# Attention scores computed twice, the second time with keys on partitions, the row maximum added in PSUM and the sums taken by a matrix of ones

## The chip, the cores and the metric

The kernel runs on one core of a Trainium2 chip. The metric is the device time of one execution in microseconds (us). Three executions of the kernel before gave a median of 409.12 us (408.9 to 410.25).

## The reference

One decoder layer on x of 8 batches x 128 tokens x 128 features, all in float32. In order: a bidirectional state-space (Mamba) block, residual and layer norm (x1); a cross attention of 16 heads of 8 features whose queries come from x1 and whose keys and values come from a context of 8 x 128 x 128, residual and layer norm (x2); a mixture of 8 experts with one expert a token, residual and layer norm. The part that the change touches is

```python
Q, K, V = query @ Wq.T, key @ Wk.T, value @ Wv.T      # split into 16 heads of 8
scores = einsum('bqhd,bkhd->bhqk', Qh, Kh) / sqrt(8)
attn = softmax(scores, axis=-1)
out = einsum('bhqk,bkhd->bqhd', attn, Vh) @ Wo.T
```

## The kernel before

Each engine has its own hand-written program (sync, gpsimd, scalar, tensor, vector: L315, L369, L476, L663, L997). They meet through semaphores. The eight PSUM banks are handed out by a written plan (L209 to L238): each entry names a tile and its bank, TensorE waits in `to_fill` until the bank's last tile was read, readers wait in `to_read`, and `filled` and `was_read` count both sides.

The scan of the state-space block takes most of the time and ends at about 254 us of the span. Then come the first norm, the attention, the routing (gate logits, counts, slots), the scatter of tokens to memory by GpSimd (L465), the experts, the gather (L471) and the last norm.

The attention has 16 tiles, i = 0 to 15: tile i is batch i // 2 and half c = i % 2 of the heads, 8 heads of 128 queries x 128 keys. The loop index i of every engine runs to LAST, and the stages of one tile lie in successive turns i. Heads are numbered h = 4 g + j: group g is a block of 32 feature rows, j one of its four heads. A head's 8 features are picked by masks: `k_maskT` holds the keys four times, each with the rows of one j only (L606), and `q_maskT` holds the queries four times, each with the rows of one g only (L1180 on VectorE, L615 on ScalarE), so one matmul of K = 128 gives four heads.

Per tile, before:

- TensorE, `scores` (L875): two matmuls of 128x128 weights and 512 columns into two banks, queries on partitions.
- VectorE, `shift_scores` (L1186): row maximum over PSUM (L1195), then scores minus maximum into SBUF (L1196).
- ScalarE (L625 to L630): eight exponentials of 128x128, each with its row sum (L628).
- VectorE, `invert_sums` (L1199): reciprocal of 8 numbers a partition (L1201). GpSimd multiplies the tile by them (L457).
- TensorE, `turn_probs` (L888): eight transposes (their line is that of the helper `turn`, L666). ScalarE copies them to SBUF (L639).
- TensorE, `weigh_values` (L895): eight matmuls of 32 output partitions each, so four lie side by side in the array (L903). For every second tile ScalarE copies the result (`evacuate`, L479) and TensorE multiplies by Wo (L957). VectorE adds the residual (L1256) and takes the moments (L1156, L1157).

In TensorE's program each float32 matmul shows as two passes, each with its own weight load, and a transpose as one.

The routing follows: `normalize` (L1162), transposes and logits (L918), `choose_expert` (L1206), `count_tokens` (L921), `place_tokens` (L1221). Among the lines of other stages that are used below are L745 (four projections with 9 rows of weights, each from its own block of 32 partitions), L727 (the matmuls behind them), L1047 (a copy of 8 numbers a partition), L1168 (the residual of the first norm) and L1070 (the start of VectorE's work after the convolution).

## Time and profile before

| | us |
|---|---|
| median of 3 executions (lowest, highest) | 409.12 (408.9, 410.25) |
| the profiled execution | 410.48 |
| its span, first to last instruction | 408.6 |
| TensorE / VectorE / ScalarE / GpSimd busy | 311.5 / 294.2 / 264.6 / 233.7 |
| mean granted TensorE clock (1 is 2.4 GHz) | 0.901 |

The durations below come from the one profiled execution. Engines are PE (TensorE matmuls), PEld (its weight loads), DVE (VectorE), ACT (ScalarE), POOL (GpSimd), SP (SyncE). Busy time is no measure of what bounds a stage: that is read from the chain of waits and from who stands idle.

### The profile page before, as it was taken

What the parts mean: (1) busy time and instruction counts of PE and PEld (TensorE: products, weight loads), DVE (VectorE), ACT (ScalarE), POOL (GpSimd) and SP (SyncE); (2) the same over time, 40 slices, a digit from 0 to 9 for tenths busy, and PEclk for the clock granted to TensorE, in tenths of its full rate; (3) what the DMA queues carried; (4) which work ended last, traced back from release to release, by engine and by line L of the source; (5) the groups of instructions that cost most, each with busy time, mean ns of one, the idle gap of its engine ahead of it and who ended that gap; (6) DMA issues with size and microseconds to landing.
All of it is one profiled execution on the core that took longest, in us unless ns stands there. A gap on an engine that the chain in (4) does not pass through costs nothing.

```text
span 408.6 us, 5591 instructions
## 1 busy us (share of the span) xinstructions
PE 311.5 (76%) x1688; PEld 189.0 (46%) x1688; DVE 294.2 (72%) x454; ACT 264.6 (65%) x677; POOL 233.7 (57%) x148
## 2 busy tenths in 40 slices
PE   4999400589999999899999999978899965249800
PEld 3443200564545555445555454834466654239700
DVE  2540579679999999999999997769777745301335
ACT  3348761059999999899999996459899972003200
POOL 7100499349888888888888882115445451700063
PEclk9999655599999999999999999999999998559955
DMA  7966001103323333222222100000000000120122
GB/s 172 315 180 209 0 1 52 51 2 103 103 105 103 109 103 105 102 92 88 97 97 97 48 2 1 2 2 0 2 1 2 3 2 0 45 72 16 34 54 65
DMA packets 16769, 26.92 MB, mean 66 GB/s; under 512 B 1964, under 2 KB 10308, under 8 KB 16740
## 3 DMA queue, kind: packets, MB, share of 16 engines
q1 hardware_dynamic: 16036, 25.46, 19.6%
q0 software_dynamic: 704, 1.10, 1.0%
q8 instruction: 14, 0.23, 0.2%
q14 instruction: 15, 0.12, 0.1%
HBM read 24.00 MB, written 2.56 MB: 65 GB/s over the span
## 4 chain that ended last, share of the span: by engine, by line
DVE 41%; PE 34%; issue 8%; ACT 7%; POOL 4%; DMA 3%; DVEq 1%; POOLq 0%; SPq 0%; ACTq 0%
DVE arena L1104 26%; PE bank L666 10%; PE bank L884 5%; DVE acc L1114 5%; PE bank L705 3%; PE bank L978 3%; PE bank L752 2%; ACT arena L628 2%; DVE delta L1085 2%; PE bank L986 2%; PE bank L957 2%; POOL dispatched_tokens L465 2%; PE bank L694 2%; POOL arena L471 2%; PE bank L903 2%
## 5 line engine op out<-in xcount | busy, mean ns | idle before, releaser
L435 POOL TENSOR_TENSOR arena<-arena,k_maskT 128x1024 f32<-128x1024 f32 x64 | 152.8, 2408 | 29.1 <-DVE arena L1104 29.1
L1104 DVE TENSOR_TENSOR_SCAN arena<-bank,arena 128x512 f32<-128x512 f32 x128 | 146.5, 1213 | 0.0
L666 PE MATMUL bank<-ident,arena 128*128 128x128 f32 (+1 forms) x686 | 103.0, 285 | 30.4 <-DVE arena L1104 11.1
L666 PEld LDWEIGHTS bank<-ident,arena 128*128 128x128 f32 (+1 forms) x686 | 75.2, 142 | 97.6 <-DVE arena L1104 60.9
L557 ACT ACTIVATE bank<-delta,a_neg 128x508 f32<-128x508 f32 x128 | 88.5, 692 | 29.5 <-DVE arena L1104 24.4
L804 PE MATMUL bank<-conv_in_T,ident 128*128 128x512 f32 x192 | 92.8, 593 | 0.0
L568 ACT ACTIVATE conv_in_T<-bank,c_col 128x256 f32<-128x256 f32 x192 | 80.4, 473 | 11.5 <-PE bank L666 10.7
L457 POOL TENSOR_TENSOR arena<-arena,rsum 128x1024 f32<-128x1024 f32 x16 | 30.3, 1897 | 36.9 <-DVE rsum L1201 36.9
L628 ACT ACTIVATE arena<-arena 128x128 f32<-128x128 f32 x128 | 37.7, 296 | 7.0 <-DVE arena L1196 6.9
L804 PEld LDWEIGHTS bank<-conv_in_T,ident 128*128 128x128 f32 x192 | 31.6, 191 | 15.8 <-issue 15.0
L884 PE MATMUL bank<-k_maskT,uT 128*128 128x512 f32 x64 | 30.9, 607 | 1.4 <-DVE uT L1180 0.8
L1008 DVE COPY arena<-bank 128x160 f32<-128x160 f32 (+2 forms) x20 | 8.1, 433 | 31.9 <-PE bank L986 16.5
L752 PE MATMUL bank<-diag_d,uT 128*128 128x128 f32 x64 | 10.0, 334 | 26.0 <-DVE woutT L1008 26.0
L1114 DVE SCALAR_TENSOR_TENSOR acc<-bank,c_col,acc 128x256 f32<-128x256 f32 x64 | 27.6, 479 | 2.6 <-PE bank L666 2.6
L1195 DVE TENSOR_REDUCE rmax<-bank 128x8 f32<-128x1024 f32 x16 | 19.5, 1217 | 12.8 <-PE bank L666 7.4
L471 POOL DMA_INDIRECT arena<-expert_outputs,take_u x8 | 7.6, 952 | 34.4 <-DMA expert_outputs<-arena 32.3
L418 POOL TENSOR_SCALAR arena<-arena 128x1024 f32<-128x1024 f32 x2 | 7.3, 3638 | 34.8 <-ACT arena L512 34.8
L479 ACT ACTIVATE arena<-bank 128x512 f32<-128x512 f32 (+1 forms) x18 | 10.3, 578 | 22.8 <-PE bank L666 18.6
L628 ACT ACTIVATION_READ_ACCUMULATOR arena<-arena 128x1 f32 x128 | 23.9, 187 | 0.0
L752 PEld LDWEIGHTS bank<-diag_d,uT 128*128 128x128 f32 x64 | 9.8, 248 | 26.4 <-issue 26.4
L1196 DVE TENSOR_TENSOR arena<-bank,rmax 128x1024 f32<-128x1024 f32 x16 | 19.6, 1224 | 0.5
L639 ACT ACTIVATE arena<-bank 128x1024 f32<-128x1024 f32 x16 | 16.1, 1004 | 2.0 <-PE bank L666 2.0
(155 smaller groups left out, 343.7 us busy)
## 6 DMA issues: line engine op xcount, KB each, us to landing
k_maskT<-b_rows SPq DMA_DIRECT2D x32, 512.0 KB, 3.7
w_sb<-in_L_ffn_w SPq DMA_DIRECT2D x1, 2048.0 KB, 10.3
dispatched_tokens<-zeros SPq DMA_DIRECT2D x1, 640.0 KB, 15.6
expert_outputs<-arena SPq DMA_DIRECT2D x4, 160.0 KB, 2.1
x_tok<-in_x SPq DMA_DIRECT2D x1, 512.0 KB, 3.9
ctx_tok<-in_ctx SPq DMA_DIRECT2D x1, 512.0 KB, 4.2
out<-arena SPq DMA_DIRECT2D x2, 256.0 KB, 2.3
arena<-dispatched_tokens SPq DMA_DIRECT2D x1, 384.0 KB, 3.8
```

Of the source, the lines that this page charges most:

```text
L435: gp.tensor_tensor(dBx[g % 2][h], du[:, dr, h, :], b_bc[:, g % RING, :], ALU.mult).then_inc(dBx_ok, 1)
L457: gp.tensor_tensor(prob[i % 3], prob[i % 3], rsum[:, i % 3, :].unsqueeze(2).to_broadcast([P, CH, S]), ALU.mult).then_inc(prob_ok, 1)
L557: sc.activation(tiles(bank[:, k % DA_BANKS, :], HB)[:, :, inner], tiles(delta[:, dr, h, half(q)], HB)[:, :, inner], ACT.Exp, scale=a_neg[: ...
L568: sc.activation(y_part[:, p, at:at + DI], hT(g, b), ACT.Copy, scale=c_col[:, dr, b, n:n + 1]).then_inc(part_ok, 1)
L628: last = sc.activation(prob[i % 3][:, h, :], prob[i % 3][:, h, :], ACT.Exp, scale=SCALE, accum_out=rsum[:, i % 3, h:h + 1])
L666: return pe.transpose(dst, src, ident[0:src.shape[0], 0:src.shape[0]])
L752: last = pe.matmul(dst[:, P * n:P * n + P], uT[:, dr, h, S * b:S * b + S], diag_d[:, dr, h, :], start=(n == 0 and dr == 0), stop=False, sk ...
L804: last = pe.matmul(bank[:, Y_BANK + p, :], ident[:, :], y_part[:, p, :], start=False, stop=False, skip_group_check=True)
L884: last = pe.matmul(bank[:, g, :], q_maskT[:, g, S * b:S * b + S], k_maskT[:, b, :, :].rearrange("p j k -> p (j k)"), start=True, stop=True)
L1104: ve.tensor_tensor_scan(o, a, v, 0.0, ALU.mult, ALU.add).then_inc(scanned, 1)
L1114: ve.scalar_tensor_tensor(acc[:, b, :], hT(g, b), c_col[:, dr, b, n:n + 1], acc[:, b, :], ALU.mult, ALU.add).then_inc(acc_ok, 1)
L1196: was_read(f"s{i}", ve.tensor_tensor(prob[i % 3], src, rmax[:, c, :].unsqueeze(2).to_broadcast([P, CH, S]), ALU.subtract))
```

## The change

The softmax is built so that the probabilities come out with keys on partitions, as the product with V needs them.

- The scores of `scores` serve the maximum alone. Their operands are now blocks of 32 partitions (`rows_g`) of an unmasked `qT` (in place of `q_maskT`, L157) and of `k_maskT`, so K = 32. They use banks 0 and 1 for every tile, where before tiles alternated between two pairs.
- VectorE takes the row maxima only (`row_maxima`). TensorE transposes them (`turn_max`, one transpose a tile) and ScalarE copies them negated to `neg_max`.
- TensorE computes the scores again, keys on partitions (`shifted_scores`): eight matmuls of K = 32 and 128 columns, then eight more of K = 32 that add the negated maximum of each query with weights `head_row`, whose only nonzero row is that of the head.
- ScalarE takes one exponential of 128x1024 from PSUM to SBUF.
- TensorE multiplies by V as before, and again by a 128x32 matrix of ones, which gives the sums in the layout of the output (one bank, 6, for every batch). VectorE takes the reciprocal of 128x512 sums and multiplies once a batch (`divide_by_sums`).
- Gone are the shift, the masks of the queries, the products on GpSimd, the eight transposes a tile and their copies. The output product moves a turn later, and the routing of the first half moves into the loop. A few constants are made at the start on VectorE and before the attention on GpSimd.

```diff
-        plan += [("x1T0", 6), ("q0", 4), ("x1T1", 7), ("s0", 0, 2), ("q1", 7), ("s1", 2, 2)]
+        plan += [("x1T0", 6), ("q0", 4), ("x1T1", 7), ("q1", 5)]
+        for i in range(LAST + 1):
+            if i < TILES_A:
+                plan += [(f"s{i}", 0, 2)]
+            if 1 <= i <= TILES_A:
+                plan += [(f"m{i - 1}", 7)]
+            if 2 <= i < TILES_A + 2:
+                plan += [(f"e{i - 2}", 2, 2)]
+            if i % 2 == 1 and 3 <= i < TILES_A + 3:
+                plan += [(f"av{i // 2 - 1}", 4 + (i // 2 - 1) % 2), (f"sum{i // 2 - 1}", 6)]
+            if i % 2 == 0 and 6 <= i < TILES_A + 6:
+                plan += [(f"wo{i // 2 - 3}", 7)]
...
# gpsimd
+            gp.memset(row_max[:, :, :, :], 0.0).then_inc(v_zero, 1)
+            gp.memset(ones_32[:, :], 1.0).then_inc(v_zero, 1)
             rstds(0)
-            for i in range(2 * B):
-                gp.wait_ge(sums_ok, i + 1)
-                gp.tensor_tensor(prob[i % 3], prob[i % 3], rsum[:, i % 3, :].unsqueeze(2).to_broadcast([P, CH, S]),
-                                 ALU.mult).then_inc(prob_ok, 1)
# scalar
+            evacuate("q1", qT[:, half(1)])
+            for i in range(1, LAST):
+                if i <= TILES_A:
+                    if i >= 3:
+                        to_read(sc, f"e{i - 3}")
+                    evacuate(f"m{i - 1}", neg_max[:, (i - 1) % 2, :], lambda ap: ap[:, 0:S], scale=-1.0)
+                if 2 <= i < TILES_A + 2:
+                    n = i - 2
+                    to_read(sc, f"e{n}")
...
+                    was_read(f"e{n}", sc.activation(probT[n % 3].rearrange("p h q -> p (h q)"),
+                                                    bank[:, 2:4, :].rearrange("p a t -> p (a t)"), ACT.Exp, scale=SCALE))
# tensor
                 for g in (2 * c, 2 * c + 1):
-                    last = pe.matmul(bank[:, g, :], q_maskT[:, g, S * b:S * b + S],
-                                     k_maskT[:, b, :, :].rearrange("p j k -> p (j k)"), start=True, stop=True)
+                    rows_g = slice(32 * g, 32 * g + 32)
+                    last = pe.matmul(bank[:, g - 2 * c, :], qT[rows_g, S * b:S * b + S],
+                                     k_maskT[rows_g, b, :, :].rearrange("p j k -> p (j k)"), start=True, stop=True)
...
+            def turn_max(i):
+                wait_read(pe, f"s{i}")
+                dst = to_fill(pe, f"m{i}")
+                filled(f"m{i}", turn(dst[:, 0:S], row_max[:, i % 2, :, :].rearrange("p g j -> p (g j)")))
+            def shifted_scores(i):
+                b, c = i // 2, i % 2
+                to_fill(pe, f"e{i}")
+                wait_read(pe, f"m{i}")
+                for j in range(GH):
+                    for g in (2 * c, 2 * c + 1):
+                        rows_g = slice(32 * g, 32 * g + 32)
+                        pe.matmul(bank[:, 2 + g - 2 * c, S * j:S * j + S], k_maskT[rows_g, b, j, :],
+                                  qT[rows_g, S * b:S * b + S], start=(j == 0), stop=False, skip_group_check=True)
+                for j in range(GH):
+                    for g in (2 * c, 2 * c + 1):
+                        rows_g = slice(32 * g, 32 * g + 32)
+                        last = pe.matmul(bank[:, 2 + g - 2 * c, S * j:S * j + S], head_row[rows_g, j, :],
+                                         neg_max[rows_g, c, :], start=False, stop=True, skip_group_check=True)
+                filled(f"e{i}", last)
...
+                for h in range(CH * c, CH * c + CH):
+                    g, j = h // GH, h % GH
+                    last = pe.matmul(total[32 * j:32 * j + 32, S * g:S * g + S], ones_32[:, :],
+                                     probT[i % 3][:, h % CH, :], start=True, stop=True)
...
             for i in range(LAST):
+                if i < TILES_A:
+                    scores(i)
+                if 1 <= i <= TILES_A:
+                    turn_max(i - 1)
+                if 2 <= i < TILES_A + 2:
+                    shifted_scores(i - 2)
+                if 3 <= i < TILES_A + 3:
                     weigh_values(i - 3)
-                if i % 2 == 1 and 5 <= i < 2 * B + 5:
-                    b = i // 2 - 2
+                if i % 2 == 0 and 6 <= i < TILES_A + 6:
+                    b = i // 2 - 3
...
+                if i == ROUTE0 + 1:
+                    count_tokens(0)
# vector
+            link(ve.tensor_reduce(one_of_32[:, :], ident[:, :].rearrange("p (g r) -> p r g", r=32)[:, 0:GH, :],
+                                  AX.X, ALU.add))
+            for j in range(GH):
+                ve.tensor_copy(head_row[:, j, :], one_of_32[:, j:j + 1].to_broadcast([P, S])).then_inc(head_row_ok, 1)
...
+            evacuate("q0", qT[:, half(0)])
+            def row_maxima(i):
+                c = i % 2
+                to_read(ve, f"s{i}")
+                ve.wait_ge(v_zero, 3)
                 if i >= 2:
+                    to_read(ve, f"m{i - 2}")
+                src = bank[:, 0:2, :].rearrange("p a (j k) -> p a j k", j=GH)
+                was_read(f"s{i}", ve.tensor_reduce(row_max[:, c, 2 * c:2 * c + 2, 0:GH], src, AX.X, ALU.max))
+            def divide_by_sums(b):
+                was_read(f"sum{b}", ve.reciprocal(inverse[:, :], to_read(ve, f"sum{b}")))
+                wait_read(ve, f"sum{b}")
+                if b >= 2:
+                    to_read(ve, f"wo{b - 2}")
+                src = to_read(ve, f"av{b}")
+                was_read(f"av{b}", ve.tensor_tensor(outT[b % 2], src, inverse[:, :], ALU.mult))
...
             for i in range(LAST + 1):
+                if i < TILES_A:
+                    row_maxima(i)
+                if i % 2 == 1 and 5 <= i < TILES_A + 5:
+                    divide_by_sums(i // 2 - 2)
                 if i % 2 == 0 and 6 <= i < TILES_A + 6:
...
+                if i == ROUTE0 - 2:
                     normalize(res2, x2, 1, 0, x2_ok)
                 if i == ROUTE0:
                     evacuate("x2T0", x2T[:, half(0)])
+                if i == ROUTE0 + 1:
+                    choose_expert(0)
+                if i == ROUTE0 + 2:
+                    place_tokens(0)
             normalize(res2, x2, 1, 1, x2_ok)
-            place_tokens(0)
```

ROUTE0 goes from 2B + 3 = 19 to 2B + 2 = 18; TILES_A is 16.

## Rows read from the trace of the kernel before

**Rows 1.** Stretches: us; busy (count) of PE, PEld, DVE, ACT, POOL; PE clock; DMA.

```profile
266.80:294.20 27.40, 22.48 (x123) 11.27 (x124) 21.34 (x29) 21.20 (x106) 10.27 (x6) 1.00 0.00 1
294.20:324.70 30.50, 30.50 (x259) 19.53 (x258) 23.02 (x37) 28.72 (x141) 15.17 (x8) 1.00 0.01 2
324.70:343.10 18.40, 13.31 (x153) 10.01 (x152) 8.54 (x23) 11.51 (x42) 6.93 (x5) 1.00 0.00 1
```

**Rows 2.** The chain of waits, two tiles of the steady stretch: start, us, what.

```profile
301.00 1.09 PE bank L957 x8
302.09 1.72 PE bank L884 x4
303.81 0.87 PE bank L666 x8
304.69 0.57 PE bank L903 x16
305.26 1.91 PE bank L884 x4
307.17 0.87 PE bank L666 x8
308.05 0.57 PE bank L903 x16
```

**Rows 3.** Groups in 266.8 to 343.1 us: count | busy us, mean ns | idle before, releasers.

```profile
L628 ACT ACTIVATE arena<-arena 128x128 f32<-128x128 f32 x128 | 37.7, 296 | 7.0 <-DVE arena L1196 6.9
...
L1195 DVE TENSOR_REDUCE rmax<-bank 128x8 f32<-128x1024 f32 x16 | 19.5, 1217 | 12.8 <-PE bank L666 7.4 <-issue 3.1 <-PE bank L884 2.3
...
L639 ACT ACTIVATE arena<-bank 128x1024 f32<-128x1024 f32 x16 | 16.1, 1004 | 2.0 <-PE bank L666 2.0
```

**Rows 4.** TensorE in order of time, 35.6 to 37.9 us.

```profile
35.66 1.14 PE L745 MATMUL bank<-rows,dtT 9*128 9x512 f32 x8
36.73 1.54 PE L727 MATMUL bank<-uT,xprojT 128*105 128x512 f32 x3
```

**Rows 5.** Single lines of VectorE: duration ns min/median/max; L1047 as a group.

```profile
L1201 DVE RECIPROCAL rsum<-rsum x16: 191/191/203, 277.2 to 332.6; 128x8 f32<-128x8 f32 x16
...
L1243 DVE RECIPROCAL route_b<-route_b x2: 178/178/179, 347.5 to 353.3; 128x4 f32<-128x4 f32 x2
...
L1047 DVE COPY vec_cols<-bank 128x8 f32<-128x8 f32 x1 | 0.2, 157 | 0.0
...
L1168 DVE TENSOR_TENSOR arena<-bank,x_tok x2: 657/674/691, 260.3 to 262.6; 128x512 f32<-128x512 f32 x2
...
332.62 0.20 DVE L1201 RECIPROCAL rsum<-rsum 128x8 f32<-128x8 f32 x1 [2.40 <-ACT arena L628]
```

**Rows 6.** In order of time, the start of the attention.

```profile
268.80 0.66 PE L666 MATMUL bank<-ident,x_tok 128*128 128x128 f32 x4 [0.85 <-DVE x_tok L1162]
...
270.21 1.95 PE L884 MATMUL bank<-k_maskT,uT 128*128 128x512 f32 x4 [0.75 <-DVE uT L1180]
...
271.25 0.60 ACT L479 ACTIVATE arena<-bank 128x512 f32<-128x512 f32 x1
...
272.20 1.22 DVE L1195 TENSOR_REDUCE rmax<-bank 128x8 f32<-128x1024 f32 x1 [2.14 <-PE bank L884]
```

**Rows 7.** VectorE in order of time, its work after the last output product.

```profile
341.62 0.69 DVE L1008 COPY arena<-bank 128x512 f32<-128x512 f32 x1 [2.11 <-PE bank L666]
342.23 0.28 DVE L1256 TENSOR_TENSOR arena<-bank,x_tok 128x128 f32<-128x128 f32 x1
...
342.87 0.18 DVE L1157 BATCH_NORM_AGGREGATE moments<-stats 128x2 f32<-128x6 f32 x1
343.53 0.19 DVE L1212 TENSOR_REDUCE route_b<-bank 128x4 f32<-128x32 f32 x1 [0.47 <-PE bank L918]
...
344.63 0.60 DVE L1162 TENSOR_SCALAR ctx_tok<-arena,moments,rstd 128x128 f32<-128x128 f32 x2
```

**Rows 8.** VectorE in order of time, its first work after the convolutions.

```profile
39.88 0.69 DVE L1070 TENSOR_SCALAR arena<-arena 128x1024 f32<-128x1024 f32 x1 [14.53 <-ACT arena L512]
```

More of the change, by code:

```diff
@@ L155, in decoder_layer_kernel @@
         x1T = arena[:, 9, :]
-        q_maskT = uT[:, :, :, :].rearrange("p a h t -> p (a h) t")
-        prob = [arena[:, c, :].rearrange("p (h k) -> p h k", h=CH) for c in range(3)]
-        probT = [arena[:, 3 + c, :].rearrange("p (h k) -> p h k", h=CH) for c in range(2)]
-        outT = [arena[:, 6, BANK * c:BANK * c + BANK] for c in range(2)]
+        qT = uT[:, 0, 0, :]
+        probT = [arena[:, c, :].rearrange("p (h q) -> p h q", h=CH) for c in range(3)]
+        inverse = arena[:, 3, 0:BANK]
+        outT = [arena[:, 4, BANK * c:BANK * c + BANK] for c in range(2)]
         res2 = arena[:, 8, :].rearrange("p (b d) -> p b d", b=B)
@@ L609, in _ @@
                          lambda ap: tiles(ap, HB * HEADS))
-            sc.wait_ge(q_first_ok, 1)
-            src = to_read(sc, "q0")
-            for g in range(2, HEADS // GH):
-                last = sc.activation(q_maskT[:, g, half(0)], src, ACT.Copy, scale=group_mask[:, g:g + 1])
-            was_read("q0", last)
             evacuate("x1T1", x1T[:, half(1)])
@@ L898, in weigh_values @@
                 wait_read(pe, f"v{b // HB}")
-                wait_read(pe, f"pT{i}")
-                dst = bank[:, where[f"av{b}"][0], :] if c else to_fill(pe, f"av{b}")
+                wait_read(pe, f"e{i}")
+                dst = bank[:, where[f"av{b}"][0], :]
+                total = bank[:, where[f"sum{b}"][0], :]
+                if not c:
+                    to_fill(pe, f"av{b}")
+                    to_fill(pe, f"sum{b}")
                 for h in range(CH * c, CH * c + CH):
@@ L903, in weigh_values @@
                     last = pe.matmul(dst[32 * j:32 * j + 32, S * g:S * g + S], v_pad[:, b, h, :],
-                                     probT[c][:, h % CH, :], start=True, stop=True)
-                if not c:
+                                     probT[i % 3][:, h % CH, :], start=True, stop=True)
+                if c:
+                    filled(f"av{b}", last)
+                for h in range(CH * c, CH * c + CH):
+                    g, j = h // GH, h % GH
+                    last = pe.matmul(total[32 * j:32 * j + 32, S * g:S * g + S], ones_32[:, :],
+                                     probT[i % 3][:, h % CH, :], start=True, stop=True)
+                if c:
+                    filled(f"sum{b}", last)
+                else:
                     last.then_inc(av_half, 1)
-                else:
-                    filled(f"av{b}", last)
             def gate_logits(g):
@@ L1175, in _ @@
             normalize(res1, x1, 0, 1, x1_ok)
-            def mask_queries(th, groups):
-                src = to_read(ve, f"q{th}")
-                for g in groups:
-                    last = ve.tensor_scalar(q_maskT[:, g, half(th)], src, group_mask[:, g:g + 1], None, ALU.mult)
-                return last
-            mask_queries(0, range(2)).then_inc(q_first_ok, 1)
-            def shift_scores(i):
+            evacuate("q0", qT[:, half(0)])
+            def row_maxima(i):
                 c = i % 2
                 to_read(ve, f"s{i}")
-                src = bank[:, 2 * c:2 * c + 2, :].rearrange("p a (j k) -> p (a j) k", j=GH)
-                if i >= 3:
-                    to_read(ve, f"pT{i - 3}")
+                ve.wait_ge(v_zero, 3)
                 if i >= 2:
-                    wait_read(ve, f"s{i - 2}")
-                link(ve.tensor_reduce(rmax[:, c, :], src, AX.X, ALU.max))
-                was_read(f"s{i}", ve.tensor_tensor(prob[i % 3], src, rmax[:, c, :].unsqueeze(2).to_broadcast([P, CH, S]),
-                                                   ALU.subtract))
-            def invert_sums(i):
-                ve.wait_ge(exp_ok, i + 1)
-                ve.reciprocal(rsum[:, i % 3, :], rsum[:, i % 3, :]).then_inc(sums_ok, 1)
+                    to_read(ve, f"m{i - 2}")
[8 more added lines that the diff above has]
+                was_read(f"av{b}", ve.tensor_tensor(outT[b % 2], src, inverse[:, :], ALU.mult))
             def over_e(ap):
@@ L1246, in _ @@
             for i in range(LAST + 1):
[L1247 to L1253 removed]
+                if i < TILES_A:
+                    row_maxima(i)
+                if i % 2 == 1 and 5 <= i < TILES_A + 5:
+                    divide_by_sums(i // 2 - 2)
+                if i % 2 == 0 and 6 <= i < TILES_A + 6:
                     b = i // 2 - 3
```

92 lines of the change are left out of this document (21 added, 71 removed).

## The prediction

> **What bounds the kernel now.** I read the stretches first, then the chain of waits inside them, then the groups and single lines for prices. The attention runs from about 267 to 343 us. In its middle TensorE is busy for the whole 30.50 us at full clock, while VectorE and GpSimd have slack and ScalarE is close to full [rows 1]. The chain there is TensorE alone: one period is scores 1.72, transposes 0.87, values 0.57, scores 1.91, transposes 0.87, values 0.57, output product 1.09, together 7.61 us for two tiles [rows 2]. So an operation taken from ScalarE, VectorE or GpSimd earns nothing there unless TensorE is relieved too. Only the start and the end, where TensorE idles (22.48 of 27.40 and 13.31 of 18.40 us [rows 1]), could be helped by the other engines.
>
> **Prices on TensorE.** A transpose is one pass of 0.109 us (0.87 for 8). The values are 16 passes, four side by side: 4 x 0.109 is 0.44, the row has 0.57, so entering that shape costs about 0.12. Scores behind values take 1.91 instead of 1.72: entering the full shape costs 0.19. I take 0.20 for every other change of shape. The output product is then 1.09 less 0.20, for 8 passes of 0.111 [rows 2]. Do blocks of 32 rows run side by side? Four matmuls of 512 columns from four blocks started at 35.66 and the next line started at 36.73: 1.07 us, which is one change (0.2) and two passes of 0.43, not eight [rows 4]. They do, at least with 512 columns. The granted clock stays a thing to watch, since it was 1.00 throughout [rows 1].
>
> Per turn, after:
> - Scores, K = 32, two blocks side by side: 0.20 + 2 x 0.43 = 1.06 (before 1.72 or 1.91).
> - Transpose of the maxima: 0.20 + 0.11 = 0.31. The eight transposes (0.87) go.
> - Shifted scores: 16 matmuls are 32 passes, in 16 pairs: 0.20 + 16 x 0.111 = 1.98. New. This is the one shape that no row shows (32 rows, 128 columns). Its lower bound is 0.109 a pair, which changes nothing. Above, either each pass waits for its weights, about 0.21 a pair (the 0.11 and half the cost of a change), or the blocks don't overlap, 0.22 a pair. I take 0.111, as rows 4 show overlap and rows 2 show hidden loads.
> - Values and sums: 0.12 + 8 x 0.11 = 1.0 (before 0.57).
> - Output product, every second turn: 1.09, as before.
>
> An odd turn is 4.35 and an even one 5.44, so TensorE alone needs 9.79 us for two tiles where it needed 7.61.
>
> The Trainium skill, page "TensorE: Matmul & The Clock Gate", Part 3 (row and column tiling), says that a weight load overlaps running matmuls only where the row group differs. In rows 2 the output product loads full-height weights for each of its 8 passes at 0.111 a pass, so loads of the same row group are hidden here, and the page would give the 0.21 above.
>
> **The new wait.** There is one bank for the sums. The first half of the next batch's values and sums (odd turns) must wait until the reciprocal of the last batch has read it. In VectorE's program that reciprocal stands behind the maxima of the same turn, which stand behind that turn's scores. So an odd turn can't be shorter than scores 1.06, hand-over 0.2 (270.21 + 0.2 + 1.71 of passes against 272.20 [rows 6]), maximum 1.2 [rows 3], reciprocal R, values and sums 1.0: 3.5 + R. It is longer than TensorE's own 4.35 once R is over 0.9.
>
> **R, the reciprocal of 128x512.** The rows have it only with 8 and 4 numbers. By medians, (191 - 178) / 4 is 3.3 ns a number; against a copy of 8 numbers it is (191 - 157) / 8, 4.3 ns above the copy's own 1 ns or so, 5.3 ns; and where the engine had stood waiting for it, as it had for the 4 numbers, the 8 took 203: (203 - 178) / 4 is 6.3 ns [rows 5]. The last compares like with like, so R = 0.2 + 504 x 0.0063, rounded to 3.3 us. The bounds: as cheap as any operation of 512 numbers, 0.67 [rows 5]; 3.3 ns gives 1.85; from above, all of the 203 beyond the copy's fixed 150 gives 6.6 ns, 3.5 us.
>
> With R = 3.3 an odd turn is 6.8 us, two tiles 12.2.
>
> **The sum, in the times of the trace.**
> - Start. The masks of the queries go, but the second half's queries now stand before the first scores: x1T1 turned by 269.5 [rows 6], copy 0.6 [rows 6], queries 1.0, hand-overs: turn 0 starts at 271.2, a us later than now (270.21).
> - Turns 0 and 1 are serial, as there is one pair of banks for the scores: 2 x (1.06 + 0.2 + 1.2) = 5.0. Turn 2 is 3.35, turn 3 4.35: 283.9. Turn 4: 288.3.
> - Six odd turns of 6.8 and five even ones of 5.44: 68.0. Turn 16 begins at 356.3 and takes 4.4 (no scores): 360.7.
> - Turn 17: VectorE adds and takes moments (0.8 [rows 7]), normalises (1.1), then R, then 1.0 of values: with hand-over 6.4, 367.1. Turn 18: rest of values 0.9, output 1.1, then on VectorE 0.8 and the copy 0.7 [rows 7]: 370.8.
> - Turn 19: R and the product 0.7 [rows 5]: 374.8. `choose_expert(0)` 1.1 (343.53 to 344.63 [rows 7]) and the counts 0.4 now stand before the last output product, 1.1: 377.4. Add and moments: 378.4. Before, they ended at 343.05 [rows 7]: 35.3 later.
> - Then `place_tokens(0)` (about 2.1) stands before the last normalisation where GpSimd's 1.6 did: 0.4 more. Scatter, experts and gather follow unchanged.
>
> That is +35.7 us. **Costed at nothing**: the five small operations of VectorE at the start, whose cover is 14.53 us of idleness (without it 1.5 us) [rows 8]; two memsets of GpSimd, which waits there for the moments; ScalarE's turn, one small copy and one exponential of 1.0 against eight of 0.296 with their sums and a copy [rows 3]. SP's queue is not touched. With R hidden it would be 8 x (3.3 - 0.9) less: 6 odd turns, turn 17 and turn 19 carry it.
>
> The profiled execution, 410.5 (span 408.6 and 1.9 around it), goes to 446; it lies 1.4 above the median, so from 409.1 I forecast 445.
>
> **Rivals.**
> - A, the forecast: R of 2.7 to 3.6 and pairs of blocks side by side, 440 to 448. Chance 0.53.
> - B, a short reciprocal, up to 2.2 us. The medians of 191 and 178 speak for it. With 1.85 it is 12 less, 433; at 0.9 and below TensorE bounds, 425. Chance 0.20.
> - C, a long reciprocal: eight ordinary steps a number. An ordinary number costs about 1.04 ns (1024 in 1.2 us [rows 3], less the fixed part), so eight are 8.3 ns, R = 4.4, 9 us more, 454. Against it: 8 numbers would lie 33 ns above 4, and lie 13 to 25 above. Chance 0.09. The Trainium skill, page "VectorE: DVE Perf Modes", "First, the fixed hardware budget", says that the reciprocal runs its divide steps with a repeat count of 8.
> - D, the pairs aren't side by side at 128 columns, or wait for their weights. Loads exposed: 1.6 more in turns 2, 3, 4 and the even ones up to 16, nine in all (in odd turns it hides in R), 0.1 more in each turn's scores: +16, 461. No overlap: 9 x 1.8 and 16 x 0.86: +30, 475. Chance 0.10.
> - E, faster. TensorE's changes of shape cost nothing with small weights, and a pair of 32-row passes takes half a pass (0.055). The even turn is then 0.86 + 0.11 + 0.88 + 0.88 + 0.89 = 3.6 and the odd one 3.6 + 0.2 at the least, if R is 0.7: 7.5 for two tiles, below 7.61, and it decides only there. With the shorter end (turns 17 to 19 in 8 us instead of 16.7) about 406. Rows 2 show changes at 0.12 to 0.20 and rows 4 a full 0.43 for a pass of few rows. Chance 0.02.
> - The rest, such as a clock that falls in TensorE's 2.5 us waits: 0.06, on the slow side.
>
> **How the numbers follow.** About 0.3% (1.2 us) can be told from no change. The likeliest case gives 445. The range is 421 to 461: it takes in B, A, C and the first half of D; outside are E, the worse half of D and most of the rest. Slower 0.97, same 0.01, faster 0.02.
>
> **What would show it.** In the changed profile: eight reciprocals of 128x512 of about 3.3 us; TensorE waiting some 2.5 us before the first half of the values in odd turns, its releaser the reciprocal; 12.2 us for two tiles, 5.4 of them the even turn; no busy GpSimd; ScalarE at about 1.3 us a tile. Wrong if the reciprocals are below 2.2 us, if TensorE has no gap in mid-stretch, if shifted scores take over 2.5 us, if the granted clock is under 1.00 between 272 and 370, or if the last moments lie before 365.

## The result, and the profile after

The changed kernel takes 486.71 us (median of 4 runs, 483.79 to 488.73) against 409.01 (408.72 to 410.25): a ratio of 1.1875, 95% interval 1.183 to 1.192. The forecast was 445, with 461 as its upper end: slower was right, the size was not, and the time lies 26 us outside the range. The profiled execution took 483.79 us, with a span of 482.0; its own forecast was 446. TensorE's mean granted clock over the span fell from 0.90 to 0.81. Of two kernels below (one full-height product more, and the first scores at full height with the ring kept) three runs in four are 1.5 to 2.2% longer than the fourth, so differences from these two are taken from their fastest run.

The stretches of the attention, cut where the granted clock changes. The columns are the stretch, its length, then busy time and instructions of the engines, the granted clock, and DMA:

```profile
core 0: us, PE busy (x) PEld busy (x) DVE busy (x) ACT busy (x) POOL busy (x), PEclk, DMA share, GB/s
266.80:272.10 5.30, 3.57 (x11) 1.03 (x11) 1.55 (x2) 0.91 (x3) 0.00 (x0) 1.00 0.00 0
272.10:313.00 40.90, 39.38 (x323) 28.01 (x325) 11.06 (x9) 6.71 (x11) 0.00 (x0) 0.50 0.00 1
313.00:319.90 6.90, 4.46 (x71) 3.22 (x73) 5.87 (x6) 1.30 (x2) 0.00 (x0) 0.99 0.01 2
319.90:330.10 10.20, 10.20 (x79) 7.55 (x81) 1.55 (x3) 1.30 (x2) 0.00 (x0) 0.50 0.01 2
330.10:336.90 6.80, 4.36 (x71) 3.11 (x71) 5.63 (x5) 1.30 (x2) 0.00 (x0) 1.00 0.00 0
```

Before, this stretch had 1.00 throughout [rows 1]. Now the clock falls to its lower level (1.2 GHz) at 272.1, four us after the first scores. It stays there for 41 us, and then goes up and down once per pair of tiles. To the last moments at 415.3 it is at half for 102 us. "PE busy" hides it: a pass at half clock counts as busy for about twice as long (the scores of a turn are 2.01 us below, where the forecast has 1.06).

The chain of waits, first at half clock, then at full clock (start, length, what; the lines are the scores L873, transposed maxima L657, shifted scores L890, maximum added L895, values L911, sums L917, output product L972, reciprocal L1209). It answers to [rows 2]:

```profile
286.26 2.01 PE bank L873 x4
288.27 0.41 PE bank L657
288.68 2.01 PE bank L890 x16
290.69 1.71 PE bank L895 x16
292.39 1.01 PE bank L911 x16
293.40 0.85 PE bank L917 x16
...
310.88 2.01 PE bank L972 x8
312.88 1.18 PE bank L873 x4
...
315.23 3.36 DVE arena L1209
318.59 0.14 issue
318.72 0.64 PE bank L911 x16
319.37 0.44 PE bank L917 x16
```

The turn at half clock takes 8.00 us (286.26 to 294.26); the forecast has 4.35 for its work. The odd turn at full clock, from 312.88 to 319.80, is the forecast's: 6.92 against 6.8, with the maximum and the reciprocal in it.

The groups of the attention, 268 to 420 us (count | busy, mean ns | idle before, releaser), and all reciprocals as single lines; they answer to [rows 3, 5]:

```profile
L890 PE MATMUL bank<-uT,k_maskT 32*128 32x128 f32 x256 | 27.7, 379 | 0.0
L1205 DVE TENSOR_REDUCE row_max<-bank 128x8 f32<-128x1024 f32 x16 | 19.6, 1224 | 39.9 <-PE bank L873 39.9
L635 ACT ACTIVATE arena<-bank 128x1024 f32<-128x1024 f32 x16 | 16.4, 1025 | 46.5 <-PE bank L895 46.5
...
L1209 DVE RECIPROCAL arena<-bank x8: 3347/3347/3349, 297.5 to 407.0; 128x512 f32<-128x512 f32 x8
  PE bank L911: 16.1, 7
```

The reciprocal takes 3.347 us and TensorE's values wait for it seven times, 16.1 us in all. Apart from that VectorE and ScalarE stand idle for TensorE (39.9 us before the maxima, 46.5 before the exponentials). The start and the end, in order of time, answer to [rows 6, 7]:

```profile
268.15 1.13 PE L873 MATMUL bank<-k_maskT,uT 32*128 32x512 f32 x4
270.60 1.13 PE L873 MATMUL bank<-k_maskT,uT 32*128 32x512 f32 x4 [1.33 <-DVE row_max L1205]
...
273.06 1.22 PE L873 MATMUL bank<-k_maskT,uT 32*128 32x512 f32 x2 [1.07 <-DVE row_max L1205]
...
415.12 0.18 DVE L1175 BATCH_NORM_AGGREGATE moments<-stats 128x2 f32<-128x6 f32 x1
```

The account of the miss, for the profiled execution against its forecast of 446 (+37.8): the attention began at 268.15 instead of 271.2, because the scans ahead of it, which the change doesn't touch, ended 3.05 us sooner in this execution (-3.05); from its first scores to the last moments it took 147.15 us instead of 107.2 (+40.0); what follows took 66.7 instead of 65.95 (+0.75). The whole miss is inside the attention, and there the work and the waits are those forecast; the clock is not.

### The profile page after: what moved, and what is told of

Same layout as the page of the kernel before. It is cut to its first block, busy times and chain, and to the rows that moved or that the text cites. A ratio compares the mean times of both kernels' runs of the same rounds, so it can differ in the third digit from the quotient of the medians.

```text
span 482.0 us, 6663 instructions
## 1 busy us (share of the span) xinstructions
PE 367.8 (76%) x2344; PEld 237.7 (49%) x2344; DVE 302.4 (63%) x437; ACT 227.0 (47%) x428; POOL 203.6 (42%) x134
## 4 chain that ended last, share of the span: by engine, by line
DVE 40%; PE 39%; issue 10%; ACT 3%; POOL 2%; DMA 2%; DVEq 1%; POOLq 0%; SPq 0%; ACTq 0%
DVE arena L1122 22%; PE bank L657 6%; PE bank L873 5%; DVE arena L1209 5%; DVE acc L1132 4%; PE bank L890 4%; PE bank L972 3%; PE bank L895 3%; PE bank L911 3%; PE bank L696 3%; PE bank L917 2%; PE bank L994 2%; PE bank L743 2%; DVE delta L1103 2%; PE bank L1002 2%
## 5 line engine op out<-in xcount | busy, mean ns | idle before, releaser
L657 PE MATMUL bank<-ident,arena 128*128 128x128 f32 (+1 forms) x558 | 85.7, 286 | 23.6 <-DVE arena L1122 11.1
L657 PEld LDWEIGHTS bank<-ident,arena 128*128 128x128 f32 (+1 forms) x558 | 60.5, 142 | 82.5 <-DVE arena L1122 60.9
L1205 DVE TENSOR_REDUCE row_max<-bank 128x8 f32<-128x1024 f32 x16 | 19.6, 1224 | 39.9 <-PE bank L873 39.9
L635 ACT ACTIVATE arena<-bank 128x1024 f32<-128x1024 f32 x16 | 16.4, 1025 | 46.5 <-PE bank L895 46.5
L481 ACT ACTIVATE neg_max<-bank 128x128 f32<-128x128 f32 x16 | 4.4, 278 | 62.5 <-PE bank L657 62.5
L873 PE MATMUL bank<-k_maskT,uT 32*128 32x512 f32 x64 | 26.9, 929 | 2.4 <-DVE row_max L1205 2.4
L890 PE MATMUL bank<-uT,k_maskT 32*128 32x128 f32 x256 | 27.7, 379 | 0.0
L911 PE MATMUL bank<-arena,delta 128*32 128x128 f32 x256 | 15.2, 376 | 16.1 <-DVE arena L1209 16.1
L1209 DVE RECIPROCAL arena<-bank 128x512 f32<-128x512 f32 x8 | 26.8, 3347 | 0.0
L895 PE MATMUL bank<-neg_max,head_row 32*128 32x128 f32 x256 | 25.5, 361 | 0.0
L890 PEld LDWEIGHTS bank<-uT,k_maskT 32*128 32x128 f32 x256 | 23.7, 272 | 3.0 <-issue 2.0
```

The lines of the kernel that those rows point to most:

```text
L657: return pe.transpose(dst, src, ident[0:src.shape[0], 0:src.shape[0]])
L873: last = pe.matmul(bank[:, g - 2 * c, :], qT[rows_g, S * b:S * b + S], k_maskT[rows_g, b, :, :].rearrange("p j k -> p (j k)"), start=True, ...
L890: pe.matmul(bank[:, 2 + g - 2 * c, S * j:S * j + S], k_maskT[rows_g, b, j, :], qT[rows_g, S * b:S * b + S], start=(j == 0), stop=False, sk ...
L895: last = pe.matmul(bank[:, 2 + g - 2 * c, S * j:S * j + S], head_row[rows_g, j, :], neg_max[rows_g, c, :], start=False, stop=True, skip_gr ...
L911: last = pe.matmul(dst[32 * j:32 * j + 32, S * g:S * g + S], v_pad[:, b, h, :], probT[i % 3][:, h % CH, :], start=True, stop=True)
L1209: was_read(f"sum{b}", ve.reciprocal(inverse[:, :], to_read(ve, f"sum{b}")))
```

## The experiments

Two theories at first. **R**: passes of 32 rows work too little of the array, and that lowers the clock. **I**: idle waits of TensorE lower it. Neither alone held. "Low" below means of 32 rows, "full height" of 128, and "the ring" the circle in which the values of an odd turn wait for the reciprocal, it for the maximum, and that for the scores. In the texts of the second four runs R stands for low passes with waits between them (in two of them for low passes alone), F for a fall that the first turns decide, G for waits at any height. In the last four B is low passes and waits together, S says that full-height first scores are enough, and L blames low passes alone or the length of the ring. B came out of the first eight runs. The kernel before took 409 to 411 us (medians) beside all of them.

**The reciprocal's cost taken away.**

```diff
-                was_read(f"sum{b}", ve.reciprocal(inverse[:, :], to_read(ve, f"sum{b}")))
+                was_read(f"sum{b}", ve.tensor_copy(inverse[:, :], to_read(ve, f"sum{b}")))
```

> The reciprocal of 128x512 becomes a copy of 128x512 (about 0.7 us instead of 3.35); the output is then not divided by the sums. TensorE's waits for it (16.1 us in the changed kernel) go. Theory R (the granted clock follows how much of the array the passes use; passes of 32 rows count as little): the clock stays at its lower level for much of the attention, mean granted clock between 280 and 360 us at most 0.75, time 450 to 485 us. Theory I (the clock falls because TensorE stands idle in gaps, at the start and for the reciprocal): with the gaps gone the clock stays at 1.00 after about 285 us, two tiles take 9.8 us and the time is 420 to 430 us.

Measured: 442.84 us (441.07 to 442.89), ratio 1.079 (1.072 to 1.085). The stretches from the fall on:

```profile
274.80:312.30 37.50, 37.50 (x318) 26.52 (x315) 7.42 (x7) 6.51 (x10) 0.00 (x0) 0.50 0.00 1
312.30:360.00 47.70, 47.70 (x730) 35.87 (x730) 21.32 (x34) 13.02 (x20) 1.27 (x2) 1.00 0.01 2
```

The clock still falls in the first turns, and stays down for 37.5 us in which TensorE is busy without a break. Then it comes back and stays at 1.00 for the same 32-row passes. So low passes don't bring it down again where no waits stand between them, and the waits of the ring are not what makes it fall first. The time lies between the ranges of R and I.

**The kernel before, with 32-row scores.**

```diff
-                    last = pe.matmul(bank[:, g, :], q_maskT[:, g, S * b:S * b + S],
-                                     k_maskT[:, b, :, :].rearrange("p j k -> p (j k)"), start=True, stop=True)
+                    rows_g = slice(32 * g, 32 * g + 32)
+                    last = pe.matmul(bank[:, g, :], q_maskT[rows_g, g, S * b:S * b + S],
+                                     k_maskT[rows_g, b, :, :].rearrange("p j k -> p (j k)"), start=True, stop=True)
```

> The kernel before, with only its scores on blocks of 32 partitions (two side by side) instead of 128 rows of masked operands; same result, half the passes' time on TensorE for the scores. TensorE's work for two tiles falls from 7.6 to 6.1 us, ScalarE's is about 7.1. Theory R: the clock falls below 1.00 in stretches of the attention and the time rises by more than 5 us. Theory I: TensorE has no gap above 1.5 us, the clock stays at 1.00, and the time falls by 2 to 4 us (ScalarE becomes the bound).

Measured: 410.25 us, ratio 1.0007 (0.9974 to 1.0041). The fall of the first turns is there without the rest of the change:

```profile
266.80:274.90 8.10, 4.83 (x18) 1.65 (x18) 6.38 (x8) 4.37 (x20) 0.00 (x0) 1.00 0.00 0
274.90:288.60 13.70, 13.59 (x68) 7.41 (x68) 10.92 (x16) 11.00 (x63) 7.37 (x4) 0.50 0.00 1
288.60:343.00 54.40, 43.59 (x460) 29.10 (x452) 37.71 (x79) 44.38 (x205) 25.47 (x17) 1.00 0.01 1
```

Two tiles take 7.2 us once the clock is back (7.61 before [rows 2]): TensorE is relieved, and VectorE's and ScalarE's work is the chain there. What that should gain doesn't show in the time; that the 14 us at half clock took it back is likely and not shown. R wanted 5 us more, I a clock of 1.00; TensorE had waited 1.7 us when it fell:

```profile
275.01 2.08 PE L885 MATMUL bank<-k_maskT,uT 32*128 32x512 f32 x4 [1.70 <-DVE arena L1197]
```

**All attention products of the changed kernel on 128 rows.**

```diff
-                        pe.matmul(bank[:, 2 + g - 2 * c, S * j:S * j + S], k_maskT[rows_g, b, j, :],
-                                  qT[rows_g, S * b:S * b + S], start=(j == 0), stop=False, skip_group_check=True)
+                        pe.matmul(bank[:, 2 + g - 2 * c, S * j:S * j + S], k_maskT[:, b, j, :],
+                                  q_maskT[:, g, S * b:S * b + S], start=(j == 0), stop=False, skip_group_check=True)
...
-                        last = pe.matmul(bank[:, 2 + g - 2 * c, S * j:S * j + S], head_row[rows_g, j, :],
-                                         neg_max[rows_g, c, :], start=False, stop=True, skip_group_check=True)
+                        last = pe.matmul(bank[:, 2 + g - 2 * c, S * j:S * j + S], head_one[:, GH * g + j, :],
+                                         neg_max[:, c, :], start=False, stop=True, skip_group_check=True)
```

The same for `scores`, with the queries masked by group as before.

> The changed kernel with both score products and the added maximum on all 128 rows (masked queries, one row of ones among 128), so none of its passes runs beside another; the same result with about twice the array time for these products. Theory R: the clock is 1.00 in the steady stretch, two tiles take about 15.3 us instead of 17.8, the time falls to 460 to 472 us. Theory I: the gaps are still there, the clock is at half for most of it, two tiles take 25 us or more, the time is above 530 us.

Measured: 472.92 us, ratio 1.154 (1.148 to 1.161), which is 14 us faster than the changed kernel although the shifted scores and the maximum added cost twice as much. The clock:

```profile
280.00:390.00 110.00, 102.35 (x1105) 84.41 (x1107) 51.87 (x53) 20.27 (x30) 1.27 (x2) 1.00 0.01 1
```

The first turns, with nearly the same waits as in the changed kernel (1.3 and 1.2 us against 1.3 and 1.1), have 1.00 too:

```profile
271.76 1.98 PE L878 MATMUL bank<-k_maskT,uT 128*128 128x512 f32 x4 [1.32 <-DVE row_max L1216]
...
275.06 1.12 PE L878 MATMUL bank<-k_maskT,uT 128*128 128x512 f32 x2 [1.21 <-DVE row_max L1216]
```

I, with over 530 us, is out. But between these waits TensorE is also at work for longer (1.98 us of scores against 1.13), so the run doesn't say whether the rows count or the time at work. Later the waits for the reciprocal are only 1.0 us here, so the steady turns don't separate height from waiting.

**One full-height product more a turn**, ahead of the shifted scores, in the changed kernel.

```diff
+                pe.matmul(bank[:, 2, :], k_maskT[:, b, 0, :], k_maskT[:, b, :, :].rearrange("p j k -> p (j k)"),
+                          start=True, stop=True)
```

> The changed kernel with one useless matmul of 128 rows, 128 weights columns and 512 columns added in each turn before the shifted scores (0.86 us at full clock, 1.7 at half; it is overwritten). Theory R: it lifts the clock, and 16 more matmuls make the kernel faster, 445 to 475 us. Theory I: the gaps stay as they are, the clock does not rise, and the time grows by 8 to 20 us.

Measured: 498.26 us (488.97 to 499.5). In the profiled execution, of 499.5 us, the clock falls at 277.2 and stays down for 68 us of unbroken work:

```profile
277.20:345.50 68.30, 68.30 (x483) 43.32 (x479) 17.31 (x15) 9.12 (x14) 0.00 (x0) 0.50 0.00 1
```

R expected 445 to 475 us and is refuted in this form: even the fastest run is 2 us over the changed kernel's median. But that run's mean granted clock is 0.829, against 0.79 to 0.81 in the changed kernel, and it is far less than the 8 to 20 us longer that I forecast, so it settles no more than that. The product doesn't stand in the first two turns, where the first waits are.

**Where the fall comes from: four runs that part the first turns from the steady ones.** The first edit puts tiles 0 to 3 on 128 rows, the second copies the sums out of PSUM, so that the reciprocal holds no bank:

```diff
+                if i < FULL:
+                    return slice(0, P), q_maskT[:, g, S * b:S * b + S]
+                return slice(32 * g, 32 * g + 32), qT[32 * g:32 * g + 32, S * b:S * b + S]
```

> The changed kernel with the attention products of tiles 0 to 3 alone (scores, shifted scores, maximum added) on all 128 rows, the other twelve tiles on 32-row blocks, and the wait for the reciprocal kept. The passes of four tiles are dearer by some 1.6 us a tile, 6 us in all. Theory F (the granted clock falls because TensorE starts the attention with 32-row passes and idle gaps between them, and once down it comes back late): the clock stays 1.00 from 268 us to about 370, two tiles take about 12.2 us (the forecast's turn), and the time is 445 + 6 = 445 to 455 us. Theory R (32-row passes with gaps between them lower the clock wherever they stand): the clock is 1.00 until about 285 and falls later, as soon as the twelve 32-row tiles run with their waits of 2.5 us; the time is 465 to 485 us.

```diff
+                if i % 2 == 1 and 5 <= i < TILES_A + 5:
+                    b = i // 2 - 2
+                    if b >= 2:
+                        to_read(sc, f"wo{b - 2}")
+                    evacuate(f"sum{b}", sums_sb[b % 2])
...
-                was_read(f"sum{b}", ve.reciprocal(inverse[:, :], to_read(ve, f"sum{b}")))
-                wait_read(ve, f"sum{b}")
+                wait_read(ve, f"sum{b}")
+                link(ve.reciprocal(inverse[:, :], sums_sb[b % 2]))
```

> The same, and ScalarE copies the row sums out of bank 6 to SBUF after every second tile, VectorE takes the reciprocal from there (nothing is left out): TensorE no longer waits for the reciprocal. At full clock two tiles take 9.8 us, seven waits of 2.4 us go (17 us from the forecast's 445), and 6 us of dearer passes come: 430 to 437 us. Theory F expects this, with the clock 1.00 from 268 to 360. Theory G (gaps lower it, whatever the height): the same. Theory R (32-row passes alone keep it low): the clock falls after 285 and stays at about 0.5 for 30 us or more as in the run with the copy, 442 to 455 us.

> The changed kernel with the sums copied to SBUF by ScalarE, all products on 32-row blocks: the wait for the reciprocal leaves the path and nothing is left out of the computation. Theory F and G: as the run with a copy in place of the reciprocal, 438 to 448 us, the clock at half from about 272 to 312 and 1.00 from there to 370, no gap of TensorE over 0.5 us for the reciprocal in 285 to 355. Rival, ScalarE in the ring: its 16 exponentials, 16 negated maxima and 8 copies (0.7 each) are 3 us a turn at most and would show as waits of shifted scores for ScalarE, 450 us or more.

```diff
-                    last = pe.matmul(bank[:, g, :], q_maskT[:, g, S * b:S * b + S],
-                                     k_maskT[:, b, :, :].rearrange("p j k -> p (j k)"), start=True, stop=True)
+                    rows_g = slice(0, P) if i < 6 else slice(32 * g, 32 * g + 32)
+                    last = pe.matmul(bank[:, g, :], q_maskT[rows_g, g, S * b:S * b + S],
+                                     k_maskT[rows_g, b, :, :].rearrange("p j k -> p (j k)"), start=True, stop=True)
```

> The kernel before with 32-row blocks for the scores of tiles 6 to 15 alone; tiles 0 to 5 stay on all 128 rows. In the run with all sixteen tiles on 32 rows the clock fell to half from 274.9 to 288.6 us and the steady two tiles took 7.18 us against 7.61. Theory F (the fill decides): the clock stays 1.00 throughout 268 to 343, five steady pairs of tiles gain 0.43 us each, 406 to 409 us, ratio 0.990 to 0.997. Theory R (the 32-row passes lower it in any stretch): a fall of some 14 us of half clock after tile 6, 410 to 413 us.

Measured: first tiles full, ring kept, 479.02 us (1.171, 1.164 to 1.177); first tiles full and sums copied out, 438.72 (1.073, 1.068 to 1.077); sums copied out alone, 446.05 (1.091, 1.087 to 1.096); the kernel before with low scores from tile 6 on, 408.50 (0.998, 0.995 to 1.001). The stretches of the first, its chain (reciprocal L1231, scores L888, maxima turned L666, shifted L905, maximum added L911), then one stretch of each of the other three:

```profile
296.00:314.00 18.00, 14.71 (x196) 11.30 (x196) 12.10 (x10) 3.90 (x6) 0.00 (x0) 1.00 0.01 2
314.00:324.20 10.20, 10.20 (x101) 7.38 (x93) 1.47 (x2) 1.30 (x2) 0.00 (x0) 0.50 0.01 2
```

```profile
297.95 3.36 DVE arena L1231
...
302.53 1.06 PE bank L888 x4
303.59 0.26 PE bank L666
303.85 1.09 PE bank L905 x16
304.94 0.89 PE bank L911 x16
...
310.18 3.36 DVE arena L1231
```

```profile
280.00:355.00 75.00, 75.00 (x1067) 58.26 (x1069) 45.08 (x48) 23.50 (x37) 1.27 (x2) 1.00 0.01 2
```

```profile
274.70:312.20 37.50, 37.50 (x317) 26.41 (x314) 10.07 (x7) 7.71 (x12) 0.00 (x0) 0.50 0.00 1
```

```profile
280.00:339.00 59.00, 47.58 (x495) 31.20 (x493) 41.81 (x73) 50.55 (x237) 28.13 (x17) 1.00 0.01 2
```

With both cures the clock is 1.00 to the end of the attention (it falls at 364). With the first alone it holds over a first wait for the reciprocal of 0.9 us, and falls at 314.0, at the end of one of 2.4 us. With the second alone it falls in the first turns. So there are two places, both with waits of over a microsecond between low passes, and F, which has the first decide, is refuted. Whether waits of 2.4 us would lower the clock between full-height products alone is not shown: no run has such waits there. The pair of tiles from 297.95 to 310.18, ring and full clock, takes 12.23 us: the forecast's 12.2. Without the ring's waits a pair takes 9.71 (reciprocals at 317.36 and 327.07), the forecast's 9.79. 438.7 is 2 us over the range that was given for full clock. The kernel before, with its clock no longer falling, gains 0.2%, which can't be told from nothing, and its interval overlaps that of the run with all scores low, so what the fall cost there stays open. It keeps its clock over this wait, which the rule of low passes and waits doesn't explain:

```profile
290.09 1.07 PE L666 MATMUL bank<-ident,arena 128*128 128x128 f32 x8 [2.35 <-ACT arena L639]
```

**The first scores alone at full height, and the wait filled.** Two runs put only `scores` on 128 rows, with the sums copied out and with the ring kept; a third adds to the second three products in the wait:

```diff
                     to_fill(pe, f"av{b}")
+                    if b:
+                        for _ in range(3):
+                            pe.matmul(dst, k_maskT[:, b, 0, :], k_maskT[:, b, :, :].rearrange("p j k -> p (j k)"),
+                                      start=True, stop=True)
                     to_fill(pe, f"sum{b}")
```

> The kernel with the sums copied out, and the first scores alone (two products of 512 columns a turn) on all 128 rows, as the kernel before has them; the shifted scores and the maximum added stay on 32-row blocks. Full height costs these two products nothing (1.06 us a turn either way). Theory B (the clock falls where low products and gaps of TensorE come together, and the 1 us of full-height products in a turn of 4.9 counts as little): a fall at about 275 us and a return near 312, as with the sums copied out alone, 443 to 449 us. Theory S (the full-height share is enough for the first turns): the clock stays 1.00 from 268 to 360, two tiles take 9.8 us from the start, and the time is 428 to 434 us.

> The changed kernel with the first scores alone on all 128 rows and the wait for the reciprocal kept. Theory B: the clock falls in the first turns or as soon as the waits of 2.4 us begin (310 us) and then goes up and down as in the changed kernel, 465 to 487 us. Theory S: the clock stays 1.00, two tiles take 12.2 us, and the time is the forecast's 441 to 450 us.

> The run with the first scores on all 128 rows and the wait for the reciprocal kept, and in that wait, every second turn, three more products of 512 columns on all rows into the bank that the values overwrite next. They come to 2.6 us at full clock (0.86 each) and the waits were 2.7 us on average (18.7 us in seven). Nothing else changes: TensorE must wait for the same reciprocal. Theory B (the clock falls where low products and gaps of 2.5 us meet): no gap is left, the clock stays 1.00 until about 375 although TensorE does more work and the ring is as long as before; seven turns pairs at 13.0 us, 450 to 460 us, against 471 to 479 without the filling. Theory L (low products alone, or the length of the ring, lower the clock): it falls again after 300 us, and with the filling at 5.2 us at half clock the time is 480 to 500 us.

Measured: 440.73 us (1.077, 1.072 to 1.083); 478.25 us (470.77 to 478.77; the profiled execution took 478.36); 460.71 us (457.2 to 461.08; 1.123, 1.116 to 1.130). The stretches of the three, one line for the first, two for the second, one for the third:

```profile
280.00:360.00 80.00, 78.91 (x1122) 57.80 (x1118) 51.27 (x53) 25.05 (x38) 1.27 (x2) 1.00 0.01 2
```

```profile
280.00:300.50 20.50, 17.92 (x243) 12.61 (x241) 12.09 (x11) 5.20 (x8) 0.00 (x0) 1.00 0.01 2
300.50:303.90 3.40, 3.40 (x12) 1.41 (x5) 0.00 (x0) 0.00 (x0) 0.00 (x0) 0.50 0.00 0
```

```profile
280.00:385.00 105.00, 102.55 (x1203) 68.88 (x1201) 57.05 (x60) 20.55 (x31) 1.27 (x2) 1.00 0.01 2
```

The chain of the third, once through the filled wait:

```profile
310.35 2.77 PE bank L910 x6
313.12 0.57 PE bank L915 x16
...
314.13 1.91 PE bank L873 x4
```

The third does all the work of the second and 2.8 us more in each wait, and is 10 us faster: 460.71 against the second's fastest run, 470.77, and even its slowest is 9.7 below that. The second's fastest run has a mean granted clock of 0.871, the third's runs 0.902 to 0.904, so by its mean it falls in that run too. In the third no fall is left up to 385 us, and L, with 480 to 500 us, is out; the time is just over B's 450 to 460. The filling adds full-height work as well as it takes the wait away. Which of the two keeps the clock isn't parted: no run fills the wait with low products. A full-height product a turn outside the wait didn't do it (the run above). Full-height first scores are enough for the first turns (S there) and not for the waits of 2.6 us (B). They are not free, as the first text has it: 1.91 and 1.72 us a turn against 1.06, so two tiles take 10.9 us, and 440.7 is 7 us over what S expected. That was my slip; [rows 2] has the prices.

**The maximum left out.** With the sums copied out, the first scores, the maxima, their transposes and the passes that add them are removed, and the exponentials read two pairs of banks in turn.

```diff
-                if i < TILES_A:
-                    scores(i)
-                if 1 <= i <= TILES_A:
-                    turn_max(i - 1)
...
-                if i < TILES_A:
-                    row_maxima(i)
```

> The kernel with the sums copied out, and with the maximum left out of the softmax: no first scores, no maximum on VectorE, no transpose of it, no passes that add it; the exponentials are taken of the unshifted scores, in two pairs of banks. TensorE has 0.99 + 1.0 + 0.55 = 2.5 us a turn at full clock, VectorE's reciprocal, product and residual make 5.0 us for two tiles, ScalarE 1.03 a turn. At full clock two tiles take 5.1 to 5.4 us, 16 tiles 43 us instead of 78, and the time is 385 to 395 us. Theory B: with so many gaps and nothing but low passes the clock falls early; at half TensorE needs 10 us for two tiles, has no gaps left, and may or may not come back before the end at 350: 405 to 425 us. Theory F (only gaps of over 2 us count): 385 to 395 us with the clock at 1.00.

Measured: 396.55 us, ratio 0.968 (0.965 to 0.972), the only one of the kernels that beats the kernel before. The clock:

```profile
266.80:280.00 13.20, 10.94 (x215) 8.43 (x214) 5.10 (x6) 7.72 (x11) 0.00 (x0) 1.00 0.00 1
280.00:313.00 33.00, 29.20 (x552) 24.83 (x556) 24.92 (x31) 13.72 (x17) 1.27 (x2) 1.00 0.01 2
```

Every score is a 32-row product here, and the clock doesn't fall in the attention: no wait of TensorE is over 0.7 us between its first products and 313. B, with 405 to 425 us, was wrong to call these gaps; low passes with waits this short did no harm. Two tiles take 6.05 us instead of the 5.1 to 5.4 expected: the reciprocal (3.33), the product (0.70), the output product (1.17) and the residual with its moments are one chain between VectorE and TensorE. Without the maximum large scores would overflow, so it is a bound on what the maximum costs and no replacement for general inputs. A version that keeps the maximum and stays at full clock needs 9.7 us for two tiles where the kernel before needs 7.61, so by these prices this layout, as written here, can't win with it.

## Why the prediction missed

- **What bounds.** Right. TensorE bounds the attention, and the relief of ScalarE and GpSimd earns nothing (ScalarE waits 46.5 us for the shifted scores).
- **TensorE's prices at full clock.** Right. The chains of the runs with tiles 0 to 3 at full height, with the ring and without, have 1.06 for scores, 0.26 (forecast 0.31), 1.09 + 0.89 = 1.98 for shifted scores (1.98), 0.57 + 0.44 for values and sums (1.0), 1.09 for the output product. Pairs of 32-row blocks cost no more than one pass at 128 columns either. The Trainium skill, "TensorE: Matmul & The Clock Gate", Part 3 (row and column tiling), as the prediction reads its rule on weight loads, would have made a pair 0.21. The chain doesn't bear that out: it gives 1.98 us for 16 pairs with one change of shape, 0.111 a pair, as the forecast took it. Rival D is out.
- **The reciprocal.** Right: 3.347 us, forecast 3.3. The price of 6.3 ns a number from [rows 5] held over 512 numbers. There was luck in it: it rests on one execution of sixteen (203 ns), and the view names no wait before the 4 numbers that it was compared with; the medians gave 3.3. B (1.85) and C (4.4) are out.
- **The new wait.** Right: seven waits, 2.3 us each on average, at the values of odd turns, 2.44 each in five of them. The odd turn is 6.92 us at full clock, and two tiles are 12.23 in the run with the first tiles at full height. One reading was off at no cost: the rows for the hand-over of 0.2 us give 0.08 (270.21 + 0.2 + 1.71 is 272.12, and the maximum starts at 272.20).
- **The start and what follows.** Right apart from the 3.05 us that the scans gave, and 0.75 us behind. (The terms of turn 18 add up to 3.5, where the sum goes on by 3.7.)
- **The step that failed** is the one on which all prices of TensorE stand: they were read from rows at a clock of 1.00 and used for a schedule in which nothing shows that the clock stays there. The text says that the clock "stays a thing to watch" and then prices it at nothing, except for "the rest, such as a clock that falls in TensorE's 2.5 us waits: 0.06, on the slow side". That is what happened in the steady turns: the clock was at half for 102 of the attention's 147 us, and they took 40 us more than forecast. The mechanism was named, as part of a remainder with a chance of 0.06 and with no price at all, so the range ended at 461; the text's own sign of being wrong, a clock under 1.00 between 272 and 370, came true. A price could be had from the forecast's own sum: with the whole attention at half clock TensorE's 9.79 us for two tiles is 19.6 against 12.2, 7.4 more for each of eight pairs, 59 us, an estimate of the worst case near 504. The trace after has 18.6 for two tiles at half clock (294.26 to 312.88).
- **Where it falls first** is a place that I never considered: turns 0 and 1, which the prediction itself calls serial. There TensorE does 1.1 us of 32-row products and waits 1.3 and 1.1 us for the maximum, and this fall is the longest, 41 of the 102 us.

The parts of the loss, from runs: 438.7 with both places cured at some 6 us of dearer passes; 479.0 with the ring and its waits back. Of those 40 us the ring's own waits are, by an estimate, 12.23 less 9.71, 2.5 for each of seven, 17.5, and the clock's share is the rest, some 23. And from 486.7 to 446.1, copying the sums out saves more than twice the 16.1 us that TensorE waited for them.

## What to carry to other kernels

A price of TensorE is a price at a clock, and in these runs the clock followed from how the new schedule worked the array. Before a sum is trusted, look for the places where short low products (few rows) alternate with waits of over a microsecond, the serial first turns of a pipeline included, and give the case at half clock a price and a real chance. The cure is to take the wait away (a copy that frees the bank early took 40 us off) or to keep TensorE at work in it: useless full-height products in the wait made the kernel 10 us faster.

## What the runs showed of the hardware

- The granted clock fell in 32-row stretches with waits of 1.1 to 1.7 us in the first turns (changed kernel, its copies, the kernel before with low scores), and not with waits of 1.2 and 1.3 us there when the first scores had 128 rows. It fell at waits of 2.4 to 2.6 us in steady turns, also with first scores of 128 rows, and at waits of 1.6 us with one full-height product more a turn. In the attention it never fell where no wait was over 0.7 us between low passes, nor with all attention products at 128 rows and waits of 1.0 us. The full-height scores also take longer (1.98 against 1.13 us), so rows and time at work aren't parted.
- Once down it can stay down through unbroken work: 37.5 us in two runs, 40.9 with 1.5 us of waits in them, 68.3 with a full-height product more a turn, against 13.7 in the kernel before with low scores, and 10.2 us at a time later on. What ends such a stretch stays open; no run was made for it alone.
- Two runs speak against a simple rule of waits: the kernel before with low scores from tile 6 on had a wait of 2.35 us from 287.7, just past its full-height scores, and kept its clock, and both kernels before with low scores had one of 1.8 us from 324 on and kept theirs to 340 and 343. Their transposes and output products are of full height.
- 32-row products of two blocks side by side cost 0.11 us a pair of 128 columns, the same as one full-height pass, and 1.06 instead of 1.72 to 1.91 us for the scores of a turn.
